# One VectorE operation over a whole row of edges, in place of six pieces, in the packing steps of a graph network kernel

## The reference

```
all_msgs = jnp.einsum('nh,thd->ntd', h, message_W) + message_b
msg = all_msgs[src, edge_type]
messages = jax.ops.segment_sum(msg, dst, num_segments=num_nodes)
gi = messages @ gru_w_ih.T + gru_b_ih
gh = h @ gru_w_hh.T + gru_b_hh
r = sigmoid(i_r + h_r)
z = sigmoid(i_z + h_z)
n = tanh(i_n + r * h_n)
return (1.0 - z) * n + z * h
...
x = _layernorm(x + _L0_gnn_ref(...), axis=-1)
```

## Time and profile before

| | |
|---|---|
| runs | 2046.14 us median of 3 (2045.62 to 2048.99) |
| the profiled execution | 2046.9 us, its span in the trace 2045.2 us |
| mean granted TensorE clock | 0.837 |
| PE busy | 1444.7 us (71%) |
| DVE busy | 1141.5 us (56%), 4039 instructions |
| ACT busy | 606.8 us (30%) |
| POOL busy | 1518.9 us (74%), 1596 instructions |

### The profile page before, as it was taken

One profiled execution on the slowest core, in us unless ns is written; L12 is line 12 of the kernel. 1 busy time (PEld: TensorE's weight loads), 2 busy tenths in 40 slices (PEclk: granted clock), 3 DMA queues, 4 the chain that ended last, 5 costly groups with the idle time before them and its releaser, 6 DMA issues. The chain is left out here.

```text
span 2045.2 us, 36875 instructions
## 1 busy us (share of the span) xinstructions
PE 1444.7 (71%) x8011; PEld 1120.8 (55%) x8109; DVE 1141.5 (56%) x4039; ACT 606.8 (30%) x1579; POOL 1518.9 (74%) x1596
## 2 busy tenths in 40 slices
PE   2667577767777777777777677776777777777775
PEld 2555465555555555555555455555555555655554
DVE  6676355555555555555555555455555555555555
ACT  3222522323232222323232232323232322323321
POOL 7777767777777777777777777777777777777773
PEclk9767788888888888887888988888778888888878
DMA  5222222222222222222222222222222222222221
GB/s 116 54 57 62 54 57 60 64 60 63 64 60 64 60 64 60 64 60 64 60 64 64 60 64 60 64 60 64 60 63 64 60 64 60 64 60 64 64 60 32
DMA packets 96735, 127.24 MB, mean 62 GB/s; under 512 B 31075, under 2 KB 70895, under 8 KB 96710
## 3 DMA queue, kind: packets, MB, share of 16 engines
q0 software_dynamic: 50688, 103.91, 20.2%
q1 hardware_dynamic: 45842, 23.04, 4.1%
q10 hardware_dynamic: 180, 0.00, 0.0%
HBM read 120.42 MB, written 6.40 MB: 62 GB/s over the span
## 5 line engine op out<-in xcount | busy, mean ns | idle before, releaser
L575 POOL DMA_INDIRECT rows<-in_x_dram,idx x1414 | 1338.1, 946 | 442.6 <-issue 403.5
L1369 PE MATMUL agg<-onehot,rows 128*128 128x128 f32 x3134 | 598.9, 344 | 102.1 <-DMA rows<-in_x_dram,idx 65.0
L1390 PE MATMUL msg<-sums_room,w_type 128*128 128x320 f32 (+1 forms) x1568 | 497.5, 478 | 199.4 <-issue 197.7
L1369 PEld LDWEIGHTS agg<-onehot,rows 128*128 128x128 f32 x3134 | 495.2, 237 | 170.0 <-issue 158.4
L1390 PEld LDWEIGHTS msg<-sums_room,w_type 128*128 128x128 f32 x1568 | 329.4, 217 | 392.2 <-issue 308.6
L636 ACT ACTIVATE sums_room<-agg 128x512 f32<-128x512 f32 x295 | 176.1, 597 | 540.0 <-PE agg L1369 539.7
L986 DVE TENSOR_TENSOR onehot<-code_T,codes 128x640 f32<-128x640 f32 (+1 forms) x295 | 244.3, 865 | 57.1 <-PE agg L1369 56.5
L1411 PE MATMUL turn<-loops,spread 16*128 16x128 bf16 x712 | 84.5, 250 | 221.6 <-ACT loops L636 219.4
L1025 DVE TENSOR_TENSOR sums_room<-turn,x_turned 128x512 f32<-128x512 f32 x178 | 123.1, 692 | 200.8 <-PE turn L1411 200.2
L636 ACT ACTIVATE counts<-cnt 128x192 f32<-128x192 f32 x99 | 32.7, 330 | 638.7 <-PE cnt L1352 631.4
L575 POOL DMA_INDIRECT rows<-in_x_dram,src_T x153 | 163.0, 1066 | 48.2 <-issue 46.3
(11 more groups left out here) (167 smaller groups left out, 1214.4 us busy)
## 6 DMA issues: line engine op xcount, KB each, us to landing
rows<-in_x_dram,idx POOLq DMA_INDIRECT x1414, 2.5
x_next<-in_x_dram SPq DMA_DIRECT2D x97, 64.0 KB
x_tile<-in_x_dram SPq DMA_DIRECT2D x97, 64.0 KB
out_dram<-out_tile SPq DMA_DIRECT2D x97, 64.0 KB
rows<-in_x_dram,src_T POOLq DMA_INDIRECT x153, 2.5
work<-in_dst_dram SPq DMA_DIRECT2D x1, 607.5 KB
work<-in_src_dram SPq DMA_DIRECT2D x1, 607.5 KB
work<-in_edge_type_dram SPq DMA_DIRECT2D x1, 607.5 KB
```

Source lines behind the costliest of these rows:

```text
L575: nc.gpsimd.indirect_dma_start(out=to, out_offset=None, in_=x[:, :], in_offset=bass.IndirectOffsetOnAxis(ap=index, axis=0),).then_inc(done ...
L1369: last = nc.tensor.matmul(agg[c][:, ds(offs[c][k] * TYPES, CODES)], (rows_second if second else rows)[:, start + k, :], onehot[c][:, k, :] ...
L1390: nc.tensor.matmul(msg[:, 0:cols], w_type[:, t, :], sums[:, t, 0:cols], start=t == 0, stop=False, skip_group_check=True)
```

## The change

Each step of `pack` is one instruction over all its columns, where it was six of 270 (the field steps: one of 1536 where there were six of 256). It waits until the step ahead is done as a whole. `AT` counts steps in place of pieces. Nothing else changes; 30 steps times 6 are 180 DVE instructions, 30 are left.

```diff
-    PIECE = ROW_EDGES // 6
...
-        AT = {name: 6 * (n + 1) for n, name in enumerate(PACK)}
+        AT = {name: n + 1 for n, name in enumerate(PACK)}
...
-            def pack(name, make, width=6 * PIECE, size=PIECE, one_by_one=False):
-
-
-                base = AT[name] - 6
-                for i in range(6):
-                    a, b = i * size, width if i == 5 else (i + 1) * size
-                    wait_used(dve, packing, base + i if one_by_one and i else base - 6 + min(i + 2, 6) if base else 0)
-                    make(i, a, b).then_inc(packing, 1)
+            def pack(name, make, width=ROW_EDGES):
+
+                wait_used(dve, packing, AT[name] - 1)
+                make(0, 0, width).then_inc(packing, 1)
 
             def pack_slots(name, make):
-                pack(name, make, ROW_SLOTS, ROW_SLOTS // 6)
+                pack(name, make, ROW_SLOTS)
...
                 pack(f"moved{stage}", lambda i, a, b: nc.vector.copy_predicated(
                     word_row[:, a:b], moves_row[:, a + d:b + d], word_row[:, a + d:b + d]),
-                    ROW_EDGES - d, one_by_one=True)
+                    ROW_EDGES - d)
```

## The result

The changed kernel takes 2055.72 us (median of 5 runs, 2052.72 to 2056.16), the kernel before 2046.14 (5 runs, 2041.25 to 2048.99): a ratio of 1.0044, with a 95% interval of 1.0028 to 1.0061. Forecast were 2048.0 and 2041 to 2053. The profiled execution took 2054.45, its span is 2052.7 (2045.2 before), so it shows 7.5 of the 9.6 us.

What follows compares the result with a forecast made beforehand. The prediction took POOL's gathers to bound the kernel up to round 8; its terms, -4.5 - 2.8 + 1.5 + 4.6 + 1.4 + 1.7, summed to +1.9 us, giving 2048.0 with a range of 2041 to 2053.

Steps and rivals of the forecast that it cites:

- The bound: POOL's gathers set the end; its losses before 192.7 count fully, and DVE's some 12 us saved are worth nothing.
- sign against the bound: The bound is wrong if the end moves otherwise than the start of round 8's gathers, 192.8 before the change.
- The mechanism: In the packing a gather gets in at each gap between dependent steps, none inside a step; no gather over 3 us.
- round 0: Gathers beside the first steps (`rise` to `wrong`): 4.2 us lost in place of 8.7, a gain of 4.5.
- `shift` and `next`: Round 1's two steps, felt in POOL's round 2: 1.7 us lost in place of 4.5, a gain of 2.8.
- `kinds`, `low`, `word`: Three steps felt in POOL's round 2: 2.3 us lost in place of 0.8, a loss of 1.5.
- "I take 2.7": Rounds 3 to 5, `moves` and `moved`: 2.7 us lost a round in place of 1.15, a loss of 4.6 in all.
- "unlucky phases": Rival with all places at their upper ends, 3.7 in each of rounds 3 to 5: +8 us, 2054; chance 0.14.
- "Everything from round 8 on is shifted as a block": Behind round 8's start nothing changes but a common shift; the wait at 238 for ACT's indices stays at 3 us.
- the outer sums of the rivals: All places lucky with free writes: 11.6 lost, -6.6 us, chance 0.11; all upper ends: 26.1, +8 us, chance 0.14.
- free writes: Gather writes are not held up: -2.5 us with middle phases, -6.6 us (2039.5) with luck; chance of the latter 0.11.
- The other case in the prediction, in which each boundary lets a gather in: Round 0 before would have lost only 0.3, not 8.7, and the change would cost 6 us and more.

Runs made afterwards that it cites:

- Experiment 9: Changed kernel with two small memsets, each waited for, ahead of the first `moves` step of rounds 3, 4 and 5: 2056.18 us, ratio 1.0033.
- nudge: Changed kernel with one small memset, not waited for, ahead of the first `moves` step of rounds 3, 4 and 5: 2053.38 us, ratio 1.0035.
- warm: Changed kernel with twelve additional TensorE products in round 8, ahead of that round's products with the type weights: 2052.30 us, ratio 1.0029.
- step_wait: Kernel before, all steps still in six pieces, but each step waits for the whole step ahead: 2037.54 us, ratio 0.9953.
- three: Kernel before with each step in three pieces, each step waiting for the whole step ahead: 2041.24 us, ratio 0.9962.
- front_chain: Kernel before, but in the eight steps before the first round and in round 1 each piece waits for the one ahead: 2036.24 us, ratio 0.9953.
- moves_whole: Kernel before with only the seven `moves` steps as one operation each, all else in six pieces: 2049.68 us, ratio 1.0015.
- moved_whole: Kernel before with only the seven `moved` steps as one operation each, all else in six pieces: 2052.48 us, ratio 1.0035.

## Why the prediction was wrong

**The bound** was right up to round 8: the start of its gathers moved by 6.1 us with the lost time of rounds 0 to 7, and DVE's 12.4 us went nowhere. The prediction's own sign against the bound (the end moves otherwise than this start) did come up: the end of the span moved by 7.5. What bounds the kernel between rounds 8 and 10 is the chain to the indices, see below.

**The mechanism** was right: one gather a step, in at each gap of 0.03 us, none over 3 us (the longest 2.83, beyond the 1.5 to 2.3 that were forecast). A gather ends 0.81 after a step's end, forecast was 0.89.

**The terms**, forecast and measured in the profiled execution: round 0 4.2 and 4.5; `shift` and `next` 1.7 and 2.4; `kinds`, `low`, `word` 2.3 and 2.7; rounds 3 to 5 8.1 (three times 2.7) and 10.8; round 6 1.8 and 1.5; round 7 2.1 and 2.6. In all 20.2 were forecast and 24.5 measured: of the 4.3 us between them 2.7 lie in rounds 3 to 5. The step that failed is "I take 2.7" for rounds 3 to 5. It took the write's wait into account but set it from the earlier trace rows, where GpSimd's write came first and DVE waited. Started 0.51 and 0.44 after a gather in place of 0.53, `moves` came first in rounds 3 and 4, and the write waited for the first `moves` too. That adds the 0.69 us of the gather of 90.38, and the following gather starts 0.39 us into `moved` (in round 5 1.07) and waits 0.8 longer. Experiment 9, with the first `moves` behind the write, gives back 1.8 of the 2.2 us by which rounds 3 and 4 exceed round 5. How long the first write waits matters less than that it waits: it ends 0.12 after `moves` in each case, so the next gather always starts 0.39 us into `moved`. In round 3 of nudge and warm the write waited only 0.2, and the round still lost 3.6 and 3.7. The rival "unlucky phases" had this case at up to 3.7 a round and got 0.14: round 5 was as forecast, rounds 3 and 4 were beyond that end. I had also summed six middle values; five of them fell on the upper side, which is luck as far as is known. And the outer sums of the rivals use ends that the parts do not give: 1.1 and 3.7 for rounds 3 to 5 where the text derives 1.45 to 2.7, 0.6 for round 6 where it has 0.9 at the least, 1.2 and 2.6 for round 7 where it has "2.1 either way".

**"Everything from round 8 on is shifted as a block"** failed as well. It moved by 2.0 us more, through the granted clock of one run of 16 products, on the chain to the indices of round 10 that the prediction itself had named as the path there. A chain on TensorE that GpSimd waits for 3.31 us is a path with no cover: what its products lose, the end loses. In the profiled executions here the two go together: at the higher clock 45.2 to 46.8 us from round 8's to round 10's first gather (seven kernels), at the lower 47.2 to 47.7 (six kernels). Of the 7.7 us between the forecast of +1.9 and the measured 9.6 us, 4.2 are the lost time of the gathers and 2.0 this chain; 0.6 comes back behind round 10, and 2.1 is by how much the medians lie further apart than the profiled executions. In step_wait and three it is 46.8 at the higher clock of these products; there the granted clock was 0.50 all through the stretch from 14 to 30 us behind round 8's first gather (0.61 in the kernel before, 0.68 in front_chain), and the products start 1.3 us later than in the others (39.5 behind that gather, 37.9 to 38.3 there). So the clock ahead of them may cost as well; no run varied it alone.

**Reads and writes apart.** The range's lower cases rested on free writes. The Trainium skill (SBUF — State Buffer, "SBUF: two separate sides") makes a difference there that I had used only in part: an operation with two SBUF inputs shuts out only a GpSimd operation that reads, one in a two-port mode shuts it out for the whole instruction. The trace agrees: under `moved` the reads waited and a write did not (the gather of 142.00), and under `moves` the write waited too (it ended 0.12 after `moves`, in the changed kernel and in moves_whole). The other case in the prediction, in which each boundary lets a gather in, is put too low: with 0.3 in place of 8.7 for round 0 before, its sum of 1.9 becomes 10.3 and not "6 us and more". In moved_whole, where each boundary of the front let gathers in, the round had 1.3.

**What stays open** is which boundary without idle time lets a gather in. One waited over more than ten of them in the earlier trace rows; in moved_whole each passed at the first one. In the four profiles with the six-piece front I took the request of a gather at 0.05 us after its start and looked at the steps up to round 2 that are in six pieces. Gathers that asked 0.04 to 0.20 us ahead of the next piece got in there; the six that asked 0.21 to 0.33 ahead waited until the last step of the stretch, over 12 to 23 boundaries; those that asked 0.34 ahead, just behind a piece's start, lost nothing. There are exceptions: the one of the earlier trace rows asked 0.06 ahead of the next operation and waited, and in step_wait gathers that asked 0.27 ahead got in. No run varied it alone. And why the clock of round 8's products falls in some kernels is not shown, only what it costs.

## What to carry to other kernels

Where GpSimd issues the transfers that set the pace, a VectorE operation with two SBUF inputs, or at two columns a step, costs not its own time but the longest stretch in which it gives GpSimd no entry; so put real gaps (a dependence between two pieces of some 0.4 us) into such stretches rather than make the operations longer or pack them denser. Cost each place by the phase in which the two engines meet, take the bad phase wherever a few hundredths of a microsecond decide it, and don't sum middle values. And look at a wait that is left on the critical path (here 3.31 us for indices) as a chain of its own, with TensorE's clock at both levels, before you call what lies behind it a block.

## What the runs showed that I had not expected

- The same code has two outcomes: 17 gathers with 9.0 or with 1.3 us of excess, and what differs between the executions is when DVE's first step starts.
- The race is decided within some 0.01 us. Over all kernels with a whole first `moves`, at 0.381 to 0.511 us after a gather's start it held back the gather's write in all eleven cases of rounds 3 to 6 (by 0.55 to 0.69); at 0.520, 0.523, 0.536 and 0.536 it was itself held back, for some 0.25.
- The gathers fall into step with the operations. Over the five kernels in which all steps of rounds 3 to 6 are whole, the gather that starts under the first `moved` starts either 0.39 us (12 rounds, where the first `moves` had held back a write) or 1.08 us (8 rounds) after it, nothing between, and takes 2.71 to 2.85 or 2.00 to 2.14. So a round loses one of few sums, and not a middle one.
- Sixteen products on TensorE took 2.8 us at a granted clock of 1.00 and 4.9 us at 0.55, and the wait that sets the kernel's path went with them: 3.1 to 3.4 us, or 5.1 to 5.5 (step_wait and three apart, 4.6).
- An independent memset of 0.07 us did not delay the operation behind it in DVE's order; it ran beside it.
